# Context keys and values of the first attention for all heads at once, and three programs made into one

## The chip, the cores and the metric

The kernel runs on one core of a Trainium2 chip. The time is device time in microseconds (us) of one launch. TensorE (PE) does the matrix products, with its weight loads shown apart as PEld; VectorE (DVE), ScalarE (ACT) and GpSimd (POOL) do the rest; SyncE (SP) issues nearly all DMAs.

## The reference

Four residual steps over x of shape (4 sequences, 512 tokens, 512 wide), float32: an attention, a mixture of experts, a second attention and a quantised feed-forward. Only the first is touched. Cut to what matters:

```python
q = (x @ wq).reshape(B, L, 16, 128); k = (x @ wk).reshape(B, L, 4, 128); v = (x @ wv).reshape(B, L, 4, 128)
k_ctx = (h_ctx_kv @ wk_ctx).reshape(B, T, 4, 128)      # T = 64 context rows in each of 4 sequences
v_ctx = (h_ctx_kv @ wv_ctx).reshape(B, T, 4, 128)
q, k, k_ctx = rms_norm(q), rms_norm(k), rms_norm(k_ctx)
q, k = rope(q), rope(k)
k_full, v_full = concat([k_ctx, k]), concat([v_ctx, v])
out = softmax(q @ k_full.T * scale + causal) @ v_full    # 4 query heads to a key head
x = x + tanh(g_xattn[0]) * (out @ wo)                     # x in q, k, v is layernorm(x)
```

## The kernel before

The program is a row of stages with a barrier of all engines between two. The first three are `constants_stage` (loads an identity matrix, two masks and the gates, and takes the gates' tanh), `norm_transpose_stage` (loads x, normalises its 16 row tiles of 128 tokens on DVE and POOL, turns each on PE and stores it on ACT as `xT`) and `attention0_stage`.

`attention0_stage` goes through 64 slots: 4 key heads (a group of 16 slots each), in a group 4 sequences ("batches"), in a batch 4 tiles of 128 query tokens. A tile of place 0 to 3 in its batch has 192, 320, 448 or 576 keys. In each slot every engine does a fixed list of short steps; the lists are written out as strings (`PE_ORDER`, `ACT_ORDER`, `DVE_ORDER`, `POOL_ORDER`), one string for each place in the batch. A step belongs to a tile of its own: in slot s PE makes the scores of tile s (`S0` to `S3`, one for each query head, L746), turns the probabilities of tile s-1 (`P`, L793), multiplies them by the values (`V`, L803), projects tile s-2 back (`W`, L120 to L122 with `a_oth`), makes keys and values of tile s+2 (`k`, L765), its queries (`q`, L120 to L122 with `a_xch`) and turns keys and queries of tile s+1 (`K` L809, `T` L814). An engine never takes a step ahead of its order: it waits on semaphores and everything listed behind waits too.

Matmuls of queries and output are done in three passes of a rounded part and a rest. The weights' rounded part is made by ACT (`w`, L512, `a_whi`), the rest by POOL (`w`, L667, `a_wlo`); x likewise (`x`, L520 and L672). Squares for the norm of queries and keys are taken by ACT (`f`, L566), summed by DVE (`E`, L646), and POOL makes the factor and applies it (`q`, L676 to L684).

The context takes two PE steps in each batch: `C` in the slot of place 1 (L773, keys and values of the context of the next batch for this one key head), and `Y` in the slot of place 2 (L820, turns the 64 keys), with the steps `c` on ACT, DVE and POOL and `y` on ACT between. Their PSUM banks are handed out in turn with those of the other steps (`A_USE`, `TR_USE`). Ahead of the slots stand the loads, the tables of the rotation (DVE L578 to L584, once all of `tab_loaded` has landed) and slots -4 to -1, which fill the pipeline.

SP issues DMAs in program order, among them `load_piece` and `store_tern`, by which a later stage's weights are read in 256 KB pieces and turned to ternary in DVE's and ACT's `j` steps.

Of the kernel before, what the change touches and what calls it, by code (L numbers as in the profile page):

```python
# [124 lines left out]
def norm_transpose_stage(nc, stage, x, ident, x_in, xT, xn_dram):  # L125


    with ExitStack() as ctx:
        s = Scope(nc, ctx, stage)
        xn = s.sb("xn", [P, 2, D])  # L130
        stats = s.sb("stats", [P, 2, 6])
        mv = s.sb("mv", [P, 2, 2])
# [2321 lines left out]
```

## Time and profile before

| | us |
|---|---|
| median of 3 runs | 2126.61 (2123.35 to 2128.16) |
| the profiled execution, its own time | 2126.97 |
| its span, first to last instruction | 2125.2 |
| first scores of slot 0 start | 78.89 |
| first scores of slot 3 start | 122.24 |
| last scores of the first attention start | 1156.1 |

Busy shares of the span: PE 90%, PEld 64%, DVE 52%, ACT 49%, POOL 46%. A PE that is busy isn't at its peak, since matmul ends are modelled, so a stretch is judged by when steps start. All start times below count from the start of the span.

### The profile page before, as it was taken

Reading aid. Unit: us, or ns where it says so; the run is one execution under the profiler, and the core shown is the slowest. Engines: PE = TensorE matmul, PEld = TensorE weight load, DVE = VectorE, ACT = ScalarE, POOL = GpSimd, SP = SyncE. Lnnn points to the kernel's source line nnn. Section 1 sums busy time; section 2 is a strip of 40 time slices with the busy share of each in tenths; the row PEclk is TensorE's granted clock in tenths of the full one; section 3 lists DMA queues with packets and bytes.
Section 4 is the critical chain, followed back from the end, with each engine's and each line's share of the span. In section 5 each row is a group of like instructions: output and inputs, shape, how many; then the busy total and the mean of one; then the engine's idle time right before and its main releaser. Section 6 shows DMA issues by size and latency. Waiting matters only on the chain. (4 is left out here: it accounts for less than half of the span.)

```text
span 2125.2 us, 27622 instructions
## 1 busy us (share of the span) xinstructions
PE 1912.4 (90%) x9644; PEld 1360.0 (64%) x9644; DVE 1111.3 (52%) x2279; ACT 1050.3 (49%) x2303; POOL 980.0 (46%) x904
## 2 busy tenths in 40 slices
PE   3799999999999999999999799998999768859998
PEld 2567666666666666666666677777999646634443
DVE  4334434346446654455443546723444468747886
ACT  2456545654544444544454321115566256647775
POOL 1544444445445443554342100006888435537774
PEclk9999999999999999999999799999999979979999
DMA  3221211201012111111000410035889570000000
GB/s 120 65 65 48 62 35 30 65 19 55 25 35 65 45 58 28 36 46 43 16 1 1 148 55 21 21 121 167 231 224 257 144 188 1 1 0 16 21 21 26
DMA packets 112198, 139.58 MB, mean 66 GB/s; under 512 B 34864, under 2 KB 68656, under 8 KB 111872
## 3 DMA queue, kind: packets, MB, share of 16 engines
q1 hardware_dynamic: 104896, 121.06, 18.6%
q0 software_dynamic: 7168, 16.78, 3.8%
q8 instruction: 78, 1.28, 0.3%
q14 instruction: 56, 0.46, 0.1%
HBM read 104.26 MB, written 28.31 MB: 62 GB/s over the span
## 5 line engine op out<-in xcount | busy, mean ns | idle before, releaser
L672 POOL TENSOR_TENSOR a_xcl<-xT,a_xch 128x512 fp32r<-128x512 f32 x64 | 82.5, 1289 | 478.5 <-ACT a_xch L520 478.5
L803 PE MATMUL a_A<-a_pT,a_vf 128*128 128x512 f32 (+1 forms) x448 | 237.5, 612 | 1.4 <-ACT a_pT L533 1.2
L590 DVE TENSOR_REDUCE a_nmax<-a_S 128x1 f32<-128x192 f32 (+3 forms) x256 | 138.9, 553 | 186.2 <-PE a_S L747 186.1
L746 PE MATMUL a_S<-a_kT,a_qT 128*128 128x288 f32 (+3 forms) x640 | 212.2, 430 | 2.8 <-ACT a_pr_even L523 1.6
L120 PE MATMUL a_A<-a_wlo,a_xch 128*128 128x512 f32 x256 | 151.7, 593 | 31.1 <-DVE a_qb L634 23.2
L523 ACT ACTIVATE a_pr_odd<-a_S,a_nmax 128x320 f32<-128x320 f32 (+1 forms) x128 | 80.9, 633 | 185.4 <-DVE a_nmax L590 184.1
L533 ACT ACTIVATE a_pT<-a_TR 128x512 f32<-128x512 f32 (+1 forms) x224 | 132.9, 594 | 57.9 <-PE a_TR L793 57.5
L746 PEld LDWEIGHTS a_S<-a_kT,a_qT 128*128 128x128 f32 x640 | 121.1, 192 | 56.2 <-issue 28.8
L523 ACT ACTIVATE a_pr_even<-a_S,a_nmax 128x192 f32<-128x192 f32 (+1 forms) x128 | 67.0, 525 | 149.4 <-DVE a_nmax L590 149.3
L765 PE MATMUL a_A<-a_wkv,xT 128*128 128x256 f32 x512 | 134.9, 386 | 0.7 <-DMA a_wkv<-in_L_xattn_wv_dram 0.7
L1403 POOL TENSOR_TENSOR e_wlo<-expert_raw,e_whi 128x1408 fp32r<-128x1408 f32 x32 | 102.5, 3224 | 66.8 <-ACT e_whi L1476 66.8
L2274 PE MATMUL f_HH<-w12T,f_xqT 128*128 128x512 bf16 x512 | 122.1, 388 | 5.0 <-DVE f_xqT L2226 4.1
L627 DVE TENSOR_TENSOR a_otl<-a_A,a_oth 128x512 fp32r<-128x512 f32 x64 | 44.3, 692 | 157.3 <-ACT a_oth L537 157.3
L120 PE MATMUL a_A<-a_wlo,a_oth 128*128 128x512 f32 x256 | 113.1, 442 | 14.5 <-POOL a_wlo L667 8.3
L120 PE MATMUL e_GUP<-e_xgl,e_whi 128*128 128x256 f32 (+1 forms) x384 | 110.1, 287 | 5.3 <-DVE e_xgl L1519 4.5
L120 PEld LDWEIGHTS a_A<-a_wlo,a_xch 128*128 128x128 f32 x256 | 49.0, 191 | 100.6 <-issue 94.3
L2125 POOL TENSOR_TENSOR f_hg<-f_h,g 128x512 f32<-128x512 f32 x64 | 81.6, 1274 | 59.2 <-DVE f_h L2233 59.2
L121 PE MATMUL e_GUP<-e_xgh,e_wlo 128*128 128x256 f32 (+1 forms) x384 | 108.7, 283 | 0.0
L122 PE MATMUL e_GUP<-e_xgh,e_whi 128*128 128x256 f32 (+1 forms) x384 | 108.1, 281 | 0.0
L122 PE MATMUL a_A<-a_whi,a_xch 128*128 128x512 f32 x256 | 102.1, 399 | 0.0
L122 PE MATMUL a_A<-a_whi,a_oth 128*128 128x512 f32 x256 | 101.8, 398 | 0.0
L121 PE MATMUL a_A<-a_whi,a_xcl 128*128 128x512 f32 x256 | 101.6, 397 | 0.0
(368 smaller groups left out, 5115.7 us busy)
## 6 DMA issues: line engine op xcount, KB each, us to landing
a_pw<-in_L_ffn_w_dram SPq DMA_DIRECT2D x96, 256.0 KB, 2.8
expert_raw<-in_L_ffn_w_gate_dram SPq DMA_DIRECT2D x16, 704.0 KB
expert_raw<-in_L_ffn_w_up_dram SPq DMA_DIRECT2D x16, 704.0 KB
expert_raw<-in_L_ffn_w_down_dram SPq DMA_DIRECT2D x16, 512.0 KB
tern<-a_tern SPq DMA_DIRECT2D x48, 128.0 KB, 1.7
x_res<-in_x_dram SPq DMA_DIRECT2D x4, 1024.0 KB, 9.8
a_raw<-in_L_xattn_wq_dram SPq DMA_DIRECT2D x4, 1024.0 KB, 5.6
a_raw<-in_L_xattn_wo_dram SPq DMA_DIRECT2D x4, 1024.0 KB, 5.3
```

The source lines that it names most:

```text
L120: pe.matmul(out, lhs_hi, rhs_lo, start=first, stop=False)
L121: pe.matmul(out, lhs_lo, rhs_hi, start=False, stop=False)
L122: return pe.matmul(out, lhs_hi, rhs_hi, start=False, stop=last)
L523: act.activation(pr[s % 2][:, i, 0:keys(s)], pair(s, i), ACT.Exp, bias=nmax[:, s % 2, i:i + 1], accum_out=rs[:, s % 2, i:i + 1]).then_inc( ...
L533: act.activation(pT[0:rows(i), i % 2], TR[0:rows(i), TR_USE["P", t, i][0]], ACT.Copy).then_inc(pT_ready, 1)
L590: ve.tensor_reduce(nmax[:, s % 2, i:i + 1], pair(s, i), AX.X, ALU.max, negate=True).then_inc(s_max, 1)
L672: pool.tensor_tensor(xcl[:, t % 2], xT[:, :, tok(t)], xch[:, t % 2].bitcast(F32), ALU.subtract).then_inc(xlo_ready, 1)
L746: pe.matmul(bank[:, lo:hi], qT[:, t % 2, hq], kT[:, par(t), lo:hi], start=True, stop=hi < nk)
L765: last = pe.matmul(bank, xT[:, k, tok(t)], wkv[:, k].rearrange("p a n -> p (a n)"), start=k == 0, stop=k == KD - 1)
L803: last = pe.matmul(A[:, A_USE["V", t, 0][0]], vf[r, par(t), i], pT[r, i % 2], start=i == 0, stop=i == nkt - 1)
L1403: pool.tensor_tensor(wlo[e % 2][q, cs], raw[q, e % 2, cs], whi[e % 2][q, cs].bitcast(F32), ALU.subtract).then_inc(gu_lo, 1)
L2274: last = pe.matmul(HH[:, n % 2, j], xqT[:, u, j * KD + k], w12T[j][:, k, part(n)], start=k == 0, stop=k == KD - 1)
```

## The change

The two programs ahead of the attention are gone: their loads and steps are in the attention's own lists, in slots -3 to 10. The context's keys and values are made once, for all four key heads and sequences: `C` (keys) and `G` (values) are two steps each of four 512-column matmuls, `H` turns the keys, and both results are stored to DRAM (`ctx_keys`, `ctx_values`). At the second slot of a batch SP loads 64 columns of keys and 64 rows of values for the next batch. `C`, `Y`, `c` and `y` leave the repeating lists. The norm of x becomes `A` (DVE), `r` (POOL, ACT), `X` (DVE) and `R` (PE, turning): rows 0 to 3 in slot -3, one row in each later slot up to 10. Cut to its core:

```diff
-    PE_ORDER = ("S0 W0 W1 S1 W2 W3 P0 k0 S2 k1 P1 V0 q0 P2 V1 S3 P3 K V2 q1 T P4 V3 q2 V4 q3",
-                "S0 W0 W1 S1 W2 W3 P0 k0 S2 k1 C P1 V0 S3 K q0 T V1 q1 q2 q3",
-                "S0 W0 W1 S1 W2 W3 P0 k0 S2 k1 P1 Y V0 q0 S3 P2 V1 K q1 T V2 q2 q3",
-                "S0 W0 W1 S1 W2 W3 P0 k0 S2 k1 P1 V0 q0 P2 V1 S3 P3 K V2 q1 T V3 q2 q3")
...
-    POOL_ORDER = ("w x q p0 p1", "x q p0 p1 c", "w x q p0 p1", "x q p0 p1")
+    PE_ORDER = {-3: "Z0 Z1 R0 R1 R2 R3 C0 C1",
+                -2: "k0 k1 H0 q0 q1 q2 q3 H1",
+                -1: "k0 k1 G0 R K T q0 q1 q2 q3 G1",
+                0: "S0 W0 W1 S1 W2 W3 P0 k0 S2 R k1 P1 V0 q0 P2 V1 S3 P3 K V2 q1 T P4 V3 q2 V4 q3",
+                1: "S0 W0 W1 S1 W2 W3 P0 k0 S2 R k1 P1 V0 S3 K q0 T V1 q1 q2 q3",
+                2: "S0 W0 W1 S1 W2 W3 P0 k0 S2 R k1 P1 V0 q0 S3 P2 V1 K q1 T V2 q2 q3",
+                3: "S0 W0 W1 S1 W2 W3 P0 k0 S2 R k1 P1 V0 q0 P2 V1 S3 P3 K V2 q1 T V3 q2 q3"}
+    ACT_ORDER = {-3: "z0 z1 r0 r1 r2 r3 x c0",
+                 -2: "w c1 x v h0 f h1",
+                 -1: "x v d0 r k t f y d1",
+                 0: "w x e0 j0 e1 g0 j1 e2 v r g1 n g2 j2 e3 g3 k t g4 o f",
...
+    DVE_SLOT = "M0 M1 N0 D X j0 M2 N1 v N2 j1 M3 N3 B E A"
+    DVE_ORDER = {-3: "A0 A1 X0 A2 X1 A3 X2 X3 t c0 c1", -2: "v E A", -1: "v X E A", 0: DVE_SLOT, 1: DVE_SLOT, 2: DVE_SLOT, 3: DVE_SLOT}
+
+    POOL_ORDER = {-3: "r0 r1 r2 r3 x c0", -2: "w c1 x r", -1: "x q r", 0: "w x q p0 p1 r", 1: "x q p0 p1 r", 2: "w x q p0 p1 r", 3: "x q p0 p1 r"}
...
+    def row(s, ahead, i):
+        return i if s == BEGIN else s + ahead if BT <= s + ahead < PERIOD else None
...
+                sp.dma_start(ident[:], consts["ident"]).then_inc(ident_loaded, 16)
+                load_x(0)
+                sp.dma_start(ctx_raw, ctx_in.rearrange("b t d -> (b t) d").rearrange("(t p) d -> p t d", p=P)).then_inc(ctx_loaded, 16)
+                sp.dma_start(wkc, wkc_in.rearrange("(k p) n -> p k n", p=P)).then_inc(wkc_loaded, 16)
                 load_q(0)
+                sp.dma_start(wrow[:, 1], kw_in.partition_broadcast(P)).then_inc(tab_loaded, 16)
                 load_pair(0, wkv, wk_in, wv_in, wkv_loaded)
+                sp.dma_start(wrow[:, 0], qw_in.partition_broadcast(P)).then_inc(tab_loaded, 16)
+                for n in "kq":
+                    sp.dma_start(cw[n][:], consts["cos"].rearrange("(t p) d -> p t d", p=P)).then_inc(tab_loaded, 16)
+                    sp.dma_start(sw[n][:], consts["sin"].rearrange("(t p) (s d) -> p t s d", p=P, s=2)).then_inc(tab_loaded, 16)
+                for k in range(KD):
+                    sp.dma_start(wvc[k], wvc_in[k * P:(k + 1) * P]).then_inc(wvc_loaded, 16)
+                sp.dma_start(causal_in[:], consts["causal"]).then_inc(causal_loaded, 16)
+                sp.dma_start(graw[:, :, 0], g_xattn.partition_broadcast(P), allow_slow_non_contiguous=True).then_inc(gates_loaded, 16)
+                sp.dma_start(graw[:, :, 1], g_ffn.partition_broadcast(P), allow_slow_non_contiguous=True).then_inc(gates_loaded, 16)
+                for b in range(1, B):
+                    load_x(b)
+                sp.dma_start(tri[:], consts["tri"]).then_inc(tri_loaded, 16)
                 load_piece(0)
                 load_piece(1)
-                for s in range(BEGIN, SLOTS):
+                store_keys(0)
+                sp.wait_ge(ck_stored, 16)
+                load_keys(0)
+                store_keys(1)
+                sp.wait_ge(wlo_ready, 4)
+                load_o(0)
+                store_values(0)
+                sp.wait_ge(cv_stored, 16)
+                load_values(0)
+                store_values(1)
+                sp.wait_ge(ck_stored, 32)
+                sp.wait_ge(cv_stored, 32)
+                    if s % BT == 1 and live(s, BT - 1):
+                        t = batch_next(s)
+                        if t >= 2 * BT:
+                            sp.wait_ge(o_full, tile(t - BT - 1))
+                        load_keys(t // BT)
+                        load_values(t // BT)
...
+                    if name == "A" and row(s, 6, i) is not None:
+                        t = row(s, 6, i)
+                        u = t % 2
+                        if t % BT == 0:
+                            ve.wait_ge(x_loaded[t // BT], 16)
+                        ve.bn_stats(stats[:, u], x[:, t]).then_inc(x_stats, 1)
+                        ve.wait_ge(x_stats, 2 * t + 1)
+                        ve.bn_aggr(mv[:, u], stats[:, u]).then_inc(x_stats, 1)
+                        ve.wait_ge(x_stats, 2 * t + 2)
+                        ve.tensor_scalar(veps[:, u:u + 1], mv[:, u, 1:2], 1e-5, None, ALU.add).then_inc(x_var, 1)
+                    if name == "X" and row(s, 5, i) is not None:
+                        t = row(s, 5, i)
+                        u = t % 2
+                        ve.wait_ge(x_rstd, t + 1)
+                        if t > 1:
+                            ve.wait_ge(xn_turned, t - 1)
+                        ve.tensor_scalar(xn[:, u], x[:, t], mv[:, u, 0:1], rstd[:, u:u + 1], ALU.subtract, ALU.mult).then_inc(xn_ready, 1)
+                    if name == "t":
...
+                    if name == "c":
+                        ve.wait_ge(ck_sq, i + 1)
+                        ve.tensor_reduce(ssc[:, i], csq, AX.X, ALU.add).then_inc(ck_sum, 1)
+                        ve.tensor_tensor(kc[:, i], A[:, A_USE["C", i, 0][0]].rearrange("p (h d) -> p h d", h=KVH),
+                                         kw[:].unsqueeze(1).broadcast_to([P, KVH, HD]), ALU.mult).then_inc(ck_done, 1)
...
+                    if name == "c":
+                        pool.wait_ge(ck_sum, i + 1)
+                        pool.tensor_tensor(msc[:, i], ssc[:, i], heps[:, 0:KVH], ALU.add).then_inc(ck_ms, 1)
+                        pool.wait_ge(ck_ms, i + 1)
+                        pool.tensor_tensor(src[:, i], msc[:, i], mhalf[:, 0:KVH], ALU.pow).then_inc(ck_rs, 1)
+                        pool.wait_ge(ck_done, i + 1)
+                        pool.wait_ge(ck_rs, i + 1)
+                        pool.tensor_tensor(kc[:, i], kc[:, i], src[:, i].unsqueeze(2).broadcast_to([P, KVH, HD]), ALU.mult).then_inc(ck_ready, 1)
...
+                    if name == "C":
+                        pe.wait_ge(wkc_loaded, 16)
+                        pe.wait_ge(ctx_copied, i + 1)
+                        bank = bank_of_A("C", i, s, m)
+                        for k in range(KD):
+                            last = pe.matmul(bank, ctxT[:, k, i * P:(i + 1) * P], wkc[:, k], start=k == 0, stop=k == KD - 1)
+                        last.then_inc(ck_full, 1)
+                    if name == "G":
+                        pe.wait_ge(wvc_loaded, 16 * KD)
+                        bank = bank_of_A("G", i, s, m)
+                        for k in range(KD):
+                            last = pe.matmul(bank, ctxT[:, k, i * P:(i + 1) * P], wvc[k], start=k == 0, stop=k == KD - 1)
+                        last.then_inc(cv_full, 1)
+                    if name == "H":
+                        pe.wait_ge(ck_ready, i + 1)
+                        bank = bank_of_TR("H", i, 0, s, m)
+                        for h in range(KVH):
+                            last = pe.transpose(bank[:, h * P:(h + 1) * P], kc[:, i, h], ident[:])
+                        last.then_inc(ck_turned, 1)
+                    if name == "R" and row(s, 5, i) is not None:
...
-                    if name == "C":
-                        bank = bank_of_A("C", t, s, m)[:, 0:2 * HD]
-                        if t % PERIOD == 0:
-                            until(pe, wc_loaded, lambda v: 32 * (v // PERIOD + 1), t, m)
-                        for k in range(KD):
-                            last = pe.matmul(bank, ctxT[:, k, ctx_tok(t)], wc[:, k].rearrange("p a n -> p (a n)"), start=k == 0, stop=k == KD - 1)
-                        last.then_inc(c_full, 1)
...
```

POOL, from the first step on x to the first queries' norm, before: `a_msc`, `a_src` and `a_kc` are the context step `c`, `a_wlo` the rest of the query weights, `a_msq` to the last `a_qa` the norm of queries of tile 0.

```order
L672 TENSOR_TENSOR a_xcl<-xT,a_xch 128x512
L693 TENSOR_TENSOR a_msc<-a_ssc,a_heps 64x1
L695 TENSOR_TENSOR a_src<-a_msc,a_mhalf 64x1
L697 TENSOR_TENSOR a_kc<-a_kc,a_src 64x128
L667 TENSOR_TENSOR a_wlo<-a_raw,a_whi 128x512 x4
L672 TENSOR_TENSOR a_xcl<-xT,a_xch 128x512 x2
L676 TENSOR_TENSOR a_msq<-a_ssq,a_heps 128x5
L678 TENSOR_TENSOR a_srq<-a_msq,a_mhalf 128x5
L681 TENSOR_TENSOR a_qa<-a_qa,a_qb 128x640
L684 TENSOR_TENSOR a_qa<-a_qa,a_srq 128x640
```

And with the change, from the same step to the same norm; `a_rstd` is the norm of a row of x, and `a_msc`, `a_src`, `a_qT` the context step `c`, now on 128 rows and 4 heads.

```order
L680 TENSOR_TENSOR a_xcl<-xT,a_xch 128x512
L700 TENSOR_TENSOR a_msc<-a_ssc,a_heps 128x4
L702 TENSOR_TENSOR a_src<-a_msc,a_mhalf 128x4
L705 TENSOR_TENSOR a_qT<-a_qT,a_src 128x512
L675 TENSOR_TENSOR a_wlo<-a_raw,a_whi 128x512 x4
L700 TENSOR_TENSOR a_msc<-a_ssc,a_heps 128x4
L702 TENSOR_TENSOR a_src<-a_msc,a_mhalf 128x4
L705 TENSOR_TENSOR a_qT<-a_qT,a_src 128x512
L680 TENSOR_TENSOR a_xcl<-xT,a_xch 128x512
L668 TENSOR_TENSOR a_rstd<-a_veps,a_mhalf 128x1
L680 TENSOR_TENSOR a_xcl<-xT,a_xch 128x512
L684 TENSOR_TENSOR a_msq<-a_ssq,a_heps 128x5
```

The context step now stands twice, on either side of the weights' rest, and a step of the row norm stands ahead of the x tile that the queries' norm follows.

PE in slot 1, from the first turned probabilities to the turned keys, before (`a_wc` is the step `C`):

```order
L793 MATMUL a_TR<-ident_f,a_pr_even 128x128 x4
L765 MATMUL a_A<-a_wkv,xT 128x256 x2
L746 MATMUL a_S<-a_kT,a_qT 128x320
L747 MATMUL a_S<-a_causal,a_ident_b 128x128
L765 MATMUL a_A<-a_wkv,xT 128x256 x2
L773 MATMUL a_A<-a_wc,a_ctxT 128x256 x4
L793 MATMUL a_TR<-ident_f,a_pr_even 128x128 x4
L803 MATMUL a_A<-a_pT,a_vf 128x512
L746 MATMUL a_S<-a_kT,a_qT 128x320
L747 MATMUL a_S<-a_causal,a_ident_b 128x128
L809 MATMUL a_TR<-ident_f,a_qa 128x128
```

And with the change (`a_xn` is the step `R`):

```order
L822 MATMUL a_TR<-ident_f,a_pr_even 128x128 x4
L801 MATMUL a_A<-a_wkv,xT 128x256 x2
L780 MATMUL a_S<-a_kT,a_qT 128x320
L781 MATMUL a_S<-a_causal,a_ident_b 128x128
L762 MATMUL a_TR<-ident_f,a_xn 128x128 x4
L801 MATMUL a_A<-a_wkv,xT 128x256 x2
L822 MATMUL a_TR<-ident_f,a_pr_even 128x128 x4
L832 MATMUL a_A<-a_pT,a_vf 128x512
L780 MATMUL a_S<-a_kT,a_qT 128x320
L781 MATMUL a_S<-a_causal,a_ident_b 128x128
L838 MATMUL a_TR<-ident_f,a_qa 128x128
```

The four passes of the context step are gone from between the second half of `k` and the second `P`, and the four transposes of a row of x stand ahead of that half.

## Rows read from the trace of the kernel before

**Rows 1.** Windows: length, busy of PE, PEld, DVE, ACT, POOL; PEclk; DMA share, GB/s.

```profile
0.00:78.89 78.89, 35.10 (x127) 26.13 (x127) 29.17 (x88) 19.16 (x39) 23.44 (x34) 0.96 0.40 124
78.89:122.24 43.35, 37.82 (x163) 25.69 (x162) 17.82 (x46) 23.82 (x66) 26.25 (x28) 0.95 0.13 43
122.24:1169.00 1046.76, 1002.55 (x4510) 698.48 (x4509) 511.49 (x1086) 527.67 (x1353) 479.79 (x486) 0.99 0.13 38
1169.00:2125.20 956.20, 836.94 (x4848) 609.70 (x4846) 552.85 (x1060) 479.63 (x846) 450.53 (x356) 0.94 0.32 92
```

**Rows 2.** Windows of slot 5 and of slot 61, first scores to first scores.

```profile
156.99:172.44 15.45, 15.24 (x71) 11.08 (x69) 7.63 (x18) 9.14 (x28) 7.88 (x10) 1.00 0.18 53
...
1119.57:1133.30 13.73, 13.52 (x63) 9.56 (x62) 7.35 (x17) 6.33 (x18) 5.56 (x6) 1.00 0.01 1
```

**Rows 3.** Timeline, PE, slots 5 and 6: start, length, line, operation, tiles.

```profile
164.27 1.89 PE L773 MATMUL a_A<-a_wc,a_ctxT 128*128 128x256 f32 x8
165.99 0.60 PE L793 MATMUL a_TR<-ident_f,a_pr_even 128*128 128x128 f32 x4
166.52 1.12 PE L803 MATMUL a_A<-a_pT,a_vf 64*128 64x512 f32 x2
...
179.97 0.60 PE L793 MATMUL a_TR<-ident_f,a_pr_odd 128*128 128x128 f32 x4
180.50 0.27 PE L820 MATMUL a_TR<-ident_f,a_kc 64*128 64x64 f32 x1
180.61 1.07 PE L803 MATMUL a_A<-a_pT,a_vf 64*128 64x512 f32 x2
```

**Rows 4.** Timeline of the first two programs and the start of the third.

```profile
0.73 0.40 SPq L2310 DMA_DIRECT2D ident_f<-const_ident_dram  x1
...
7.51 2.60 SPq L152 DMA_DIRECT2D x_res<-in_x_dram  x4
...
13.13 1.29 DVE L175 BATCH_NORM_STATS2 n_stats<-x_res 128x6 f32 x2 [5.48 <-DMA x_res<-in_x_dram]
...
15.04 1.17 POOL L198 TENSOR_TENSOR n_rstd<-n_veps,n_mhalf 128x1 f32<-128x1 f32 x2 [14.61 <-DVE n_veps L182]
...
45.21 0.31 ACT L497 ACTIVATE a_ident_b<-ident_f 128x128 bf16<-128x128 f32 x1 [0.78 <-PEq L100]
```

**Rows 5.** Timeline from the landing of the tables to the first scores.

```profile
53.24 0.23 DVE L578 TENSOR_SCALAR a_kw<-a_sq 128x128 f32<-128x128 f32 x1 [7.51 <-DMA a_sq<-in_L_xattn_k_norm_w_dram]
...
56.44 0.63 ACT L520 ACTIVATE a_xch<-xT 128x512 fp32r<-128x512 f32 x1 [4.65 <-DVE a_sin_k L584]
...
61.13 4.98 POOL L667 TENSOR_TENSOR a_wlo<-a_raw,a_whi 128x512 fp32r<-128x512 f32 x4
...
67.16 0.60 ACT L566 ACTIVATE a_sq<-a_A 128x512 f32<-128x512 f32 x1 [4.71 <-PE a_A L122]
...
67.79 0.82 DVE L646 TENSOR_REDUCE a_ssq<-a_sq 128x5 f32<-128x640 f32 x1 [4.93 <-ACT a_sq L566]
...
69.86 1.18 POOL L678 TENSOR_TENSOR a_srq<-a_msq,a_mhalf 128x5 f32<-128x5 f32 x1
...
72.61 1.25 POOL L684 TENSOR_TENSOR a_qa<-a_qa,a_srq 128x640 f32<-128x640 f32 x1
...
73.92 0.47 PE L809 MATMUL a_TR<-ident_f,a_qa 128*128 128x128 f32 x1 [3.04 <-POOL a_qa L684]
...
78.89 0.73 PE L746 MATMUL a_S<-a_kT,a_qT 128*128 128x192 f32 x2
```

**Rows 6.** Windows of 2 KB loads, of 512-byte loads, and ahead of the first scores.

```profile
11.00:20.00 9.00, 2.17 (x9) 1.77 (x10) 5.23 (x16) 1.19 (x2) 2.34 (x4) 1.00 1.03 387
49.20:53.20 4.00, 1.96 (x8) 1.56 (x8) 0.00 (x0) 1.19 (x2) 0.00 (x0) 1.00 1.21 297
72.60:79.40 6.80, 5.48 (x16) 4.46 (x17) 0.26 (x1) 1.15 (x3) 1.25 (x1) 0.50 0.00 0
```

**Rows 7.** The page, DMA issues: the 256 KB pieces.

```profile
a_pw<-in_L_ffn_w_dram SPq DMA_DIRECT2D x96, 256.0 KB, 2.8
```

More of the change, by code:

```diff
@@ L392, in attention0_stage @@
+        ck_stored, cv_stored, ck_loaded, cv_loaded = (s_.sem(n) for n in ("ck_stored", "cv_stored", "ck_loaded", "cv_loaded"))
         q_sq, q_sum, q_rot, q_ms, q_rs, q_add, q_ready = (s_.sem(n) for n in (
             "q_sq", "q_sum", "q_rot", "q_ms", "q_rs", "q_add", "q_ready"))
-        c_ms, c_rs, c_ready = s_.sem("c_ms"), s_.sem("c_rs"), s_.sem("c_ready")
         piece_loaded = [s_.sem(f"piece_loaded{u}") for u in range(2)]
@@ L657, in _ @@
             def _(pool):
-                pool.wait_ge(tab_ready, 4 + 2 * (1 + BT))
+                pool.wait_ge(tab_ready, 2)
                 def do(name, i, s, m):
+                    if name == "r" and row(s, 6, i) is not None:
+                        t = row(s, 6, i)
+                        pool.wait_ge(x_var, t + 1)
+                        pool.tensor_tensor(rstd[:, t % 2:t % 2 + 1], veps[:, t % 2:t % 2 + 1], mhalf[:, 0:1], ALU.pow).then_inc(x_rstd, 1)
                     if name == "w" and s % PERIOD in (2, 14):
@@ L716, in bank_of_A @@
                         sem, count = {"W": (wo_done, tile), "V": (o_lo, tile), "q": (q_rot, tile), "k": (kv_done, tile),
-                                      "C": (c_done, batch)}[before[0]]
+                                      "C": (ck_done, tile), "G": (cv_copied, tile)}[before[0]]
                         until(pe, sem, count, before[1], m)
@@ L724, in bank_of_TR @@
                         sem, count = {"P": (pT_ready, turn(before[2])), "T": (qT_ready, tile), "K": (kT_ready, tile),
-                                      "Y": (cT_ready, batch)}[before[0]]
+                                      "Z": (ctx_copied, tile), "R": (xT_ready, tile), "H": (ck_copied, tile)}[before[0]]
                         until(pe, sem, count, before[1], m)
@@ L740, in do @@
                             if t % BT == 0:
-                                until(pe, cT_ready, batch, t, m)
+                                until(pe, ck_loaded, lambda v: 16 * batch(v), t, m)
+                                pe.wait_ge(tab_ready, 3)
                         until(pe, s_exp, head(i - 2), t, m)
@@ L799, in do @@
                             if t % BT == 0:
-                                until(pe, c_done, batch, t, m)
+                                until(pe, cv_loaded, lambda v: 16 * batch(v), t, m)
                         until(pe, pT_ready, turn(i), t, m)
@@ L2330, in build @@
         ident = sb(ctx, "ident_f32", [P, P])
-        causal = sb(ctx, "causal_f32", [P, P])
         tri = sb(ctx, "tri_f32", [P, P])
```

331 lines of the change are left out of this document (124 added, 207 removed), and 9 rows, old and new, of tables (ACT_ORDER, DVE_ORDER).

## Prediction

> **What bounds the kernel now.** I read the windows first, cut where the scores of slots 0 and 3 begin and where the first attention ends. From 122.24 to 1169 us PE is busy 1002.55 of 1046.76 us at a mean clock of 0.99, while no other engine reaches 530 us there [rows 1]; the reader is to see one full engine beside four half-empty ones. In this stretch a step that leaves PE is worth the distance between the starts of its neighbours. The first 78.89 us are the other kind: PE is busy 35.10 of them, and what ends a wait there is a landing, DVE or POOL in turn [rows 1, 4, 5]. The 956.20 us behind the attention are untouched. Then I read slot against slot in the windows, the lead step by step in the timeline, and the rates of loads in the windows again.
>
> **The steady slots.** The trace holds the experiment for step C. Slot 5 has it and takes 15.45 us; slot 61, the same place in its batch with no batch to follow, lacks it and takes 13.73 us [rows 2]. The difference, 1.72, is also the distance from C's first pass to the next step, 164.27 to 165.99 [rows 3]. C stands in 15 slots (1, 5, ... 57); I count 14 here and slot 1 below: 14 x 1.71 = 23.9 us gained. Slot 61 also shows that nothing else fills the place: without C it is idle only 0.21 of its 13.73 us, as slot 5 is of its 15.45 [rows 2]. What could take part of it back is the bank: the queries' first product then waits for DVE's key step of the same slot, and in the slots with ternary pieces DVE is later. Bounds: none of 1.71 lost, or all of it in the 6 such slots (10 us); slot 61 is nearest and I take none.
>
> Step Y is cheap: from the turned probabilities to the values it is 0.53 us without it (165.99 to 166.52) and 0.53 + 0.11 with it (179.97 to 180.61) [rows 3]. 14 x 0.11 = 1.5 us gained. The small steps c and y on ACT, DVE and POOL go too; these engines have spare time [rows 1], so I count them at nothing.
>
> Against that, R, A, X and r of rows 5 to 15 of x now lie in slots 0 to 10. R is four transposes as in the turning of probabilities, 0.53 us from start to next step [rows 3]; in slots 3 to 10, with PE full, 8 x 0.53 = 4.2 us lost. A is about 1 us on DVE (13.13 to 15.04 for two rows) and r 0.6 us on POOL [rows 4], at the end of a slot, ahead of the next maxima. DVE's half-empty slots [rows 1] cover them; without the cover each would delay the exponentials and so PE, at most 1 us x 8. Below, the wait where q0 waits for DVE may shrink by as much as R adds; I keep 4.2, between 0 and 12.
>
> The loads of stored keys and values are issued by SP three slots ahead of their use. A 256 KB piece lands 2.8 us after its issue [rows 7], a slot lasts 13.7 to 15.5 us [rows 2], so I count them at nothing.
>
> **The lead.** Before: 78.89 us to the first scores. After, on the order of each engine:
>
> 1. Data. One queue brings everything in program order. Up to the causal mask, for which DVE's table step waits, stand 4.5 MiB in 2 KB rows (first quarter of x, context, three weights) and 1.75 MiB in 512-byte rows. At 387 and 297 GB/s [rows 6] these are 12.2 and 6.2 us. The lead of a load: x is issued from 7.51 and its first MiB is there at 13.13 [rows 4]; 5.6 less 2.7 of transfer leaves 2.9. From the first issue at 0.73 [rows 4]: 0.73 + 2.9 + 18.4 = 22.0 us.
> 2. Tables: 53.24 to 56.44, 3.2 us [rows 5], so 25.2.
> 3. POOL's order, shown above, puts c0 ahead of the weights' rest. DVE sums the squares of four heads, 0.7 us (four fifths of 0.82), and multiplies; POOL's power of four columns takes about 1.0 (1.18 for five) and a product 1.25 [rows 5]. c0 ends near 28.5.
> 4. The rest of the query weights: 4.98 us [rows 5], 33.5. From its end to the squares of the queries it was 67.16 - 66.11 = 1.05 [rows 5], so f starts at 34.5.
> 5. From f to the end of the queries' norm it was 67.16 to 73.86, 6.7 us [rows 5]. Now POOL first takes c1 (0.2 + 1.0 + 1.25, to 36), an x tile, and then r of row 4, for which DVE's E and A must end (34.5 + 0.6 + 2.0 + 1.0 = 38.2). With r 0.6 and another x tile of 1.3 the norm starts near 40 and takes 4.2: 44.3. So K starts about 3 us later than the old pattern would have it.
> 6. From K to the first scores it was 73.92 to 78.89, 4.97 us [rows 5], at half clock (0.50 in 72.6 to 79.4, the engine having waited 3.04 us for POOL ahead of it [rows 5, 6]); about 3.6 at full. G1 now lies in between: twice the columns of C, 2 x 1.72 = 3.4 us at full clock [rows 3], 6.9 at half. So the first scores start at 51.4 us with a full clock and 56.2 with a half one.
>
> The Trainium skill, "TensorE: Matmul & The Clock Gate", section Part 1 on the HAM clock gate, says that the array is throttled unless recent activity has released it. The trace agrees (0.50 behind a wait of 3.04 us), and by that rule the lead, in which PE mostly waits, would end at the later of the two times.
>
> I take 54: half of the stretch slow. H, k and G0 lie in POOL's shadow; if POOL were quicker, G0 (3.4) would come into the path. Gain 78.89 - 54 = 24.9 us, bounds 22.7 and 27.5. Slots 0 to 2 took 43.35 us [rows 1]. They lose C once but gain three R, and A delays the maxima in slot 1, where PE already waits; I take 0.8 us lost, from 2 gained to 4 lost.
>
> **Sum.** 24.9 - 0.8 + 23.9 + 1.5 - 4.2 = 45.3 us. The profiled execution took 2126.97 us, 0.36 above the median of 2126.61, so 2081.7 by the one and 2081.3 by the other; I write 2081.
>
> **Rivals.** First, the setup is slower than I have it: the causal mask at the end of the load queue, POOL's one list and a half clock add up, or the row norm's DVE steps reach PE in slots 1 to 10. For it: six waits in a row hang on the order of POOL and SP, and one late landing moves all. Price: 2.2 more for the later of the two leads, 3.2 for slots 0 to 2 at their bound, 4 for A in slots 3 to 10 (half of its bound), and 2.6 for a landing that comes a MiB later (1.05 MB at 387 GB/s): 2081 + 12 = 2093.
>
> Second, the setup is faster: the 512-byte rows too run at 387 GB/s (4.7 us for 6.2), the clock is full by K (2.6), and slots 0 to 2 end at their better bound (2.8). Together 7, so 2074. Against it: 297 GB/s was measured in just such a queue, and the half clock in just such a place [rows 6].
>
> Third, PE's time isn't given back, since DVE's key step ends the slot instead: the C term falls to 14 us and R stays, 2091, or at its worst 2105. Against it stands slot 61.
>
> On the other side: every batch waits for its keys. If SP, which runs one list with the pieces and ternary stores, reaches the load only when the batch is due, PE stands still at 15 batch starts for an issue and a landing, 2.8 us [rows 7]: 42 us, and 2123, no change that a measurement can tell. From 45.3 / 15 = 3.0 us each it is slower, and two loads one behind the other could cost that: 3.3 each gives 2131. Against it: the load hangs on values of a batch that ended three slots earlier, 40 us.
>
> The Trainium skill, "DMA: Bandwidth & Descriptors", section Anatomy of one DMA, puts a fixed 2 us on every DMA, and its specification table asks for 512 bytes for line rate, while a key load has 256 bytes to a partition. By its figures alone an exposed load would be an estimated 2.1 us and 15 of them 31; the 2.8 of the 256 KB pieces stands in its place here.
>
> **How the numbers follow.** The sum's own case 0.68 (2075 to 2089), slower setup 0.12, faster setup 0.10, PE's time not given back 0.05, waiting batches 0.05, of which 0.02 short of a measurable loss. Other stretches of half clock, each worth some 2 us, may move by one or two either way. The range takes in the sum, both setups and the milder end of the third: 2068 to 2095, about 0.9 of the cases by their middles, 0.8 with their spread. A measurement of this kernel can tell about 0.2%, 4 us, from no change: faster 0.95, same 0.02, slower 0.03.
>
> **What would show it.** Right: first scores near 54 us; slot 5 near 14.2 us and slot 13 near 13.7; the slots of places 0 and 3 unchanged behind slot 10; no wait of PE on `ck_loaded` or `cv_loaded`; the end of the attention some 45 us earlier and what follows as long as before. Wrong: a wait of PE ahead of the first score of a batch; slot 13 at 15.4 us; first scores beyond 60 us; the maxima of slots 3 to 10 so late that PE waits for exponentials; or another clock behind 1169 us.

## Result: faster, by half of what was predicted

The changed kernel took 2102.91 us (median of 4 runs, 2102.16 to 2105.11), the kernel before 2125.51 beside it (4 runs, 2123.35 to 2128.16): a ratio of 0.9895, interval 0.9878 to 0.9912. The prediction said 2081, with a range of 2068 to 2095; the sign was right, the gain 22.6 us in place of 45. In later series the kernel before stood at 2128.4 to 2129.3 and the changed one at 2102.2, so the gain is 23 to 27 us.

The windows of the changed kernel, cut at the first scores, at slot 3 and at the attention's end, answer to [rows 1]; the columns are the same:

```profile
0.00:55.92 55.92, 36.09 (x113) 22.84 (x114) 19.63 (x49) 15.37 (x30) 20.92 (x26) 0.88 0.67 218
55.92:104.98 49.06, 39.55 (x167) 27.01 (x165) 20.36 (x54) 24.55 (x65) 27.13 (x28) 0.90 0.14 45
104.98:1144.00 1039.02, 990.35 (x4423) 684.90 (x4422) 519.47 (x1104) 523.92 (x1306) 463.33 (x452) 0.99 0.13 37
1144.00:2101.20 957.20, 837.42 (x4841) 610.79 (x4839) 553.03 (x1060) 480.08 (x845) 450.84 (x356) 0.94 0.32 92
```

The reader sees a lead of 55.92 us for 78.89, slots 0 to 2 longer by 5.7, and a long third window only 7.7 shorter, where some 21 were expected. PE's work in it fell by 12.2 us (1002.55 to 990.35), not by the 14 x 1.7 of step C.

Yet step C is gone as predicted. The windows of slots 5 and 13 answer to [rows 2]:

```profile
141.28:155.66 14.38, 14.17 (x66) 9.96 (x65) 8.66 (x21) 9.14 (x26) 7.35 (x8) 1.00 0.19 61
273.21:287.00 13.79, 13.58 (x63) 9.57 (x61) 7.37 (x17) 6.87 (x19) 6.77 (x7) 1.00 0.15 44
```

14.2 and 13.7 were forecast. And nothing waits for the loads of stored keys and values: this is the whole list of PE's waits from 104 to 1144 us (total us, times, longest), without a DMA in it.

```profile
PE a_A L120 <- DVE a_qb L643: 26.5, 27, 1.6
PE a_A L120 <- POOL a_wlo L675: 6.1, 6, 1.9
PE a_A L120 <- issue: 5.3, 3, 1.8
PE a_A L120 <- DVE a_otl L636: 4.8, 17, 1.4
PE a_TR L843 <- ACT a_pT L526: 3.3, 16, 0.6
PE a_A L832 <- ACT a_pT L526: 1.2, 2, 0.9
PE a_TR L762 <- DVE a_xn L577: 1.1, 2, 0.6
```

Where the rest went is seen when slots are laid beside slots, before against after. Apart from step C and the rows of x, they differ only where one of the two shows half clock. Slots 24 and 32 are the same place with the same work; these are their windows in the changed kernel, and from its timeline the queries' first product in each:

```profile
454.85:474.44 19.59, 18.12 (x80) 12.82 (x79) 9.38 (x20) 7.78 (x21) 6.87 (x7) 0.91 0.14 41
593.33:611.21 17.88, 16.42 (x80) 11.85 (x79) 9.36 (x20) 7.78 (x21) 6.86 (x7) 1.00 0.15 44
```

```profile
464.22 0.47 PE L120 MATMUL a_A<-a_wlo,a_xch 128*128 128x512 f32 x1 [1.47 <-DVE a_qb L643]
...
602.68 0.47 PE L120 MATMUL a_A<-a_wlo,a_xch 128*128 128x512 f32 x1 [1.46 <-DVE a_qb L643]
```

Both slots have the wait for DVE's key product, 1.47 and 1.46 us. After the first, the granted clock is 0.50 for 3.4 us (1.2 GHz, the lower of its two levels, in place of 2.4), as a window of just this stretch shows; such stretches are called half clock below. The row above it is one of 6.8 us in slot 2, of which more below:

```profile
85.80:92.60 6.80, 5.46 (x12) 3.66 (x13) 0.70 (x2) 1.49 (x5) 6.72 (x7) 0.50 0.16 41
464.70:468.10 3.40, 3.40 (x9) 2.08 (x9) 0.61 (x1) 0.60 (x1) 0.00 (x0) 0.50 0.45 134
```

The slot's mean is 0.91, and PE is busy 1.7 us longer for the same 80 instructions; after the second it stays at full. In the kernel before both slots took 17.92 us. Before, four such stretches fell into slots 3 to 61 (14, 43, 51, 55); after, nine (24, 27, 30, 34, 46, two in 50, 52, 55).

The account from profile to profile, in us gained, with the start of slot 62 (1133.30 before, 1108.28 after) as the cut behind the slots:

| term | predicted | in the traces |
|---|---|---|
| lead, to the first scores | 24.9 | 23.0 |
| slots 0 to 2 | -0.8 | -5.7 |
| step C, 14 slots | 23.9 | 23.5 (14 x 1.68) |
| step Y | 1.5 | 0 |
| R, A, X, r in slots 3 to 10 | -4.2 | -5.0 |
| slots 3 to 61 whose clock differs | 0 | -10.4 |
| small lengthenings, up to 0.06 a slot | 0 | -0.3 |
| from slot 62 on (991.90 to 992.92) | 0 | -1.0 |
| sum (of unrounded terms) | 45.3 | 24.0 |

The -10.4 is the sum over ten slots whose clock differs: 14, 43 and 51 gained 1.47, 1.66 and 1.63; 24, 27, 30, 34, 46, 50 and 52 lost 1.67, 1.64, 1.50, 2.80, 1.55, 4.33 and 1.68. Slot 50 holds two stretches. Slots 34 and 50 lost more than their stretches because a second wait follows the first stretch there, which the kernel before does not have. These are the queries' first product of slot 34, the first ternary step (`j0`) that it waits behind, and the wait for DVE's key product in the kernel before, all slots together (27 times and 26.5 us with the change, above):

```profile
639.74 0.47 PE L120 MATMUL a_A<-a_wlo,a_xch 128*128 128x512 f32 x1 [1.62 <-DVE a_qb L643]
```

```profile
634.30 1.48 DVE L614 TENSOR_SCALAR a_below<-a_pw,a_nthr 128x512 bf16<-128x512 f32 x1
635.82 1.62 DVE L618 SCALAR_TENSOR_TENSOR a_tern<-a_pw,a_thr,a_below 128x512 bf16<-128x512 f32 x1
```

```profile
PE a_A L120 <- DVE a_qb L634: 23.2, 25, 1.5
```

In slot 34 of the kernel before the same two instructions took 0.48 and 0.75 us, and the queries' first product did not wait. Behind the half clock they start 1.2 us later in the slot and run beside POOL's products for the queries' norm; why that matters stands under "The waits away". So some 3 us of the 10.4 are these two waits, 1.62 in slot 34 and 1.42 in slot 50 (half clock follows the latter too), and the rest is the slower clock itself.

### The profile page after: what moved, and what is told of

It reads as the page before. It is cut to its first block and busy times, and to the rows that moved or that the text cites. A ratio compares the mean times of both kernels' runs of the same rounds, so it can differ in the third digit from the quotient of the medians.

```text
span 2101.2 us, 27108 instructions
## 1 busy us (share of the span) xinstructions
PE 1903.4 (91%) x9540; PEld 1345.5 (64%) x9540; DVE 1112.5 (53%) x2265; ACT 1043.9 (50%) x2245; POOL 962.2 (46%) x862
## 5 line engine op out<-in xcount | busy, mean ns | idle before, releaser
L120 PE MATMUL a_A<-a_wlo,a_xch 128*128 128x512 f32 x256 | 152.4, 595 | 32.1 <-DVE a_qb L643 26.5
L636 DVE TENSOR_TENSOR a_otl<-a_A,a_oth 128x512 fp32r<-128x512 f32 x64 | 44.3, 692 | 156.6 <-ACT a_oth L530 156.6
L801 PEld LDWEIGHTS a_A<-a_wkv,xT 128*128 128x128 f32 x512 | 89.1, 194 | 22.3 <-DVE a_qT L593 6.7
```

What stands on the lines that cost most here:

```text
L120: pe.matmul(out, lhs_hi, rhs_lo, start=first, stop=False)
L801: last = pe.matmul(bank, xT[:, k, tok(t)], wkv[:, k].rearrange("p a n -> p (a n)"), start=k == 0, stop=k == KD - 1)
```

## Experiments

All times are medians; slots with half clock are counted from 3 to 61, in one profiled execution of each kernel. Theory A: PE's longer waits are the old ones, and which of them half clock follows hangs on when they fall. Rival B: the absence of C's work brings the clock down at those places.

**A little more work at one place.** Ahead of step k in slot 12, products that the step then overwrites (n = 2, 4, 6):

```diff
+for _ in range(n if s == 12 and i == 0 else 0):
+    pe.matmul(bank, xT[:, 0, tok(t)], wkv[:, 0]..., start=True, stop=True)
```

> The changed kernel with two extra products of the first slice of x with the key and value weights in slot 12, ahead of step k, which then starts its bank afresh: 0.86 us more work on PE at one place, and the same result. Its profile should keep every wait of the changed kernel and every slot length but that of slot 12. Theory A (the waits of PE of 1.4 us and more are the old ones, and whether one of them is followed by 3.4 us of half clock hangs on the moment at which it falls): another set of slots behind slot 12 has half clock than 24, 27, 30, 34, 46, 50 (two), 52 and 55, in number 4 to 10, and the time is 2103.8 us plus 1.65 for each stretch above those 9, minus 1.65 for each below, so 2096 to 2105. Rival B (PE lost the work of step C, and its absence beside the waits brings the clock down in those places): the same slots have it, 2103.8 us, give or take 1.

> As the one before, with four extra products, 1.72 us in slot 12. Theory A: yet another set of slots with half clock, 4 to 10 of them, and 2104.6 us plus or minus 1.65 for each stretch above or below 9. Rival B: the same slots as in the changed kernel, 2104.6 us.

> As the shifts of 0.86 and 1.72 us, with six extra products, 2.58 us in slot 12. Theory A: another set of slots with half clock than in the changed kernel, 4 to 10 of them, and 2105.5 us plus or minus 1.65 for each above or below 9. Rival B: the nine of the changed kernel, 2105.5 us.

Measured 2099.6 (2099.0 to 2102.5), 2108.5 (2102.8 to 2109.1) and 2104.7 us (2100.3 to 2109.9). With 0.86 us of work added the median is 3 us lower, which the spread of the unchanged kernel's executions (2096.7 to 2108.4 us, below) does not let one call a gain. What the profile shows is where the half clock stands. The windows of its slots 24, 27 and 43:

```profile
455.32:473.24 17.92, 16.46 (x81) 11.86 (x79) 9.38 (x20) 7.76 (x21) 6.87 (x7) 1.00 0.15 45
...
503.36:524.64 21.28, 19.60 (x82) 13.54 (x81) 11.75 (x21) 9.07 (x20) 7.85 (x7) 0.92 0.12 37
...
780.50:801.74 21.24, 19.57 (x83) 13.55 (x82) 11.74 (x21) 9.07 (x20) 7.84 (x7) 0.92 0.14 38
```

Slot 24 now runs at full clock, 43 does not: six stretches (27, 30, 34, 43, 46, 50). Slot 62 starts 4.3 us earlier for it (1103.95 for 1108.28), and what follows takes 3.8 us longer (996.7 for 992.9). The third shift has five (24, 35, 43, 46, 50). The second alone speaks for B: it has the nine of the changed kernel, and another in slot 14 beside them. The first and third contradict B.

**The same kernels again.**

> The changed kernel, unchanged, profiled in another execution. Theory A: the same slots at full clock, another set with half clock than 24, 27, 30, 34, 46, 50 (two), 52 and 55, or a part of them; 5 to 10, 2098 to 2106 us. Rival B: the same nine. If the median comes out at 2102 to 2104 again, the distance to the kernel before on the same chip, 2129, is 25 to 27 us.

> The kernel before, unchanged, profiled in another execution. Theory A (which of the same waits is followed by half clock hangs on when it falls): every slot at full clock takes what it took in the first profile, within 0.05 us, but the slots with half clock behind slot 3 are not 14, 43, 51 and 55 again; between 3 and 10 of them, and the time 2121 to 2135 us. Rival B (the work beside the waits decides): the same four.

2102.2 (2096.7 to 2108.4) and 2128.4 us (2124.6 to 2137.8). The changed kernel's slots 24, 27 and 36 in this execution:

```profile
451.81:471.35 19.54, 18.09 (x81) 12.98 (x80) 9.36 (x20) 7.77 (x21) 6.86 (x7) 0.91 0.13 41
...
501.50:521.11 19.61, 17.94 (x82) 12.60 (x81) 11.73 (x21) 9.08 (x20) 7.86 (x7) 1.00 0.14 41
...
662.73:682.32 19.59, 18.14 (x81) 12.82 (x79) 9.37 (x20) 7.77 (x21) 6.87 (x7) 0.91 0.14 41
```

Slot 27 is at full clock and 36 is not; there are eight stretches (24, 30, two in 34, 36, 39, 46, 50). One program, two executions, two sets: B in its strict form is out. The kernel before changed less than A expected: 18 in place of 14, and 43, 51 and 55 again. Between these two profiles slot 62 starts 27.6 us earlier with the change (1131.34 to 1103.71), for 25.0 in the first pair.

**C's time back, without C.** The same dead products, four of them, in the 15 slots that had C (`i == 0 and 1 <= s <= 57 and s % BT == 1`).

> The changed kernel with four extra products (of x's first slice with the key and value weights, a bank that step k then starts afresh) ahead of step k in the 15 slots of place 1 that had step C: PE's time of C back, without C's loads, statistics or turning; the result is the same. Slots of place 1 return to 15.4 to 15.5 us, so 15 x 1.72 = 25.8 us more at full clock. Theory A with the spacing of the waits as what decides: the stretches in slots 3 to 62 come back to what the kernel before has, 4 to 7, and the time is 2120 to 2127 us. If the number has to do with anything else of the change: 9 or 10, 2128 to 2131.

2115.7 us (9 runs, 2107.0 to 2126.3): 25.8 us of added work cost 13.5. Slots 24, 25 and 43:

```profile
461.24:479.14 17.90, 16.45 (x81) 11.86 (x80) 9.36 (x20) 7.76 (x21) 6.86 (x7) 1.00 0.14 45
479.14:494.63 15.49, 15.28 (x71) 11.08 (x69) 10.54 (x21) 6.84 (x19) 7.32 (x7) 1.00 0.18 57
...
788.91:810.19 21.28, 19.60 (x82) 13.51 (x81) 11.75 (x21) 9.08 (x20) 7.84 (x7) 0.92 0.14 37
```

Slot 25 has its old length, and three stretches are left, in 43, 51 and 55: the very slots of both profiles of the kernel before. That points to C's time in the rhythm of the slots, and not to its loads, statistics or turning; but it is one profile, and the nine executions lie 19 us apart, at mean clocks from 0.957 to 0.968. A had expected 4 to 7 stretches. The median lies below the expected 2120 to 2127: slot 1, which waits anyway, took up its products (14.44 us, and 14.45 at full clock without them in the third shift), and the execution profiled, 2118.3, lies above the median.

**C away, and nothing else.**

```diff
-if name == "c" and live(batch_next(s), 0):
+if name == "c" and batch_next(s) < 2 * BT:
```

(the same for y, C and Y, and for the waits on them).

> The kernel before with steps C, Y, c and y left out from the third batch on, and the loads of the next heads' context weights with them (the later batches then read the contexts' keys and values of the first two, so this part of the computation is left out): the one part of the change that gave the prediction its largest term, alone, with the two programs and the lead of before. Both theories: 13 slots of place 1 fall from 15.44 to 13.76 us, 21.8 us, and the lead and slots 0 to 4 stay as they were. Theory A (which waits are followed by half clock hangs on when they fall): the number of such stretches in slots 3 to 62 differs from the 4 of before, anything from 3 to 10, and the time is 2107 us plus 1.65 for each above 4, so 2105 to 2117. Rival D (the added half clock comes from what else the change did: rows normalized beside the slots, loads of stored keys): 4 stretches, 2105 to 2107.

2112.4 us (2105.4 to 2117.0). Slots 13 and 24:

```profile
284.64:298.36 13.72, 13.51 (x62) 9.55 (x61) 7.35 (x17) 6.85 (x19) 6.75 (x7) 1.00 0.13 38
...
467.55:487.12 19.57, 18.10 (x80) 12.78 (x79) 9.38 (x20) 7.76 (x21) 6.87 (x7) 0.91 0.12 41
```

C's time is given back, and the stretches go from four to six (14, 24, 27, 30, 34, 51), 24, 27, 30 and 34 among them as in the changed kernel. Rival D, something else in the change, needed the four old ones and 2105 to 2107 us: the set and the median are against it. The execution profiled is the fastest of the five, though, and its 2105.4 us alone would fit D.

**The waits away.** In slots 24 to 55 the waits for DVE's key product come from DVE's first ternary step, which stands ahead of it. The step is long there. These are the first and the second ternary step of slot 32 in the changed kernel:

```profile
597.83 1.37 DVE L614 TENSOR_SCALAR a_below<-a_pw,a_nthr 128x512 bf16<-128x512 f32 x1
599.24 1.62 DVE L618 SCALAR_TENSOR_TENSOR a_tern<-a_pw,a_thr,a_below 128x512 bf16<-128x512 f32 x1
...
602.52 0.47 DVE L614 TENSOR_SCALAR a_below<-a_pw,a_nthr 128x512 bf16<-128x512 f32 x1
603.02 0.75 DVE L618 SCALAR_TENSOR_TENSOR a_tern<-a_pw,a_thr,a_below 128x512 bf16<-128x512 f32 x1
```

The first runs while POOL makes its products for the queries' norm (597.38 to 600.32), the second while POOL rests. In this trace all 24 ternary steps beside a resting POOL took 0.47 and 0.75 us. So the wait of 1.46 us hangs on what POOL does at the time as well as on the order; no run varied POOL alone. The step was moved back in places 0, 2 and 3 (with one wait of DVE on its own last step):

```diff
-M0 M1 N0 D X j0 M2 N1 v N2 j1 M3 N3 B E A
+M0 M1 N0 D X M2 N1 v N2 j0 j1 M3 N3 B E A
```

> The changed kernel with DVE's first ternary step of a slot (j0) moved behind the key's products and N2 in the slots of places 0, 2 and 3 (and a wait of DVE on its own last ternary step ahead of the next). In slots 24 to 55 the queries' first product waits 1.46, 0.68 and 1.5 us for DVE's key product, which stands behind j0. Theory A: without these waits 16 slots lose 0.7 to 1.5 us each, some 16 to 20 us, and the half clock that followed them in slots 24, 27, 34, 50, 52 and 55 goes too, 5 to 6 stretches of 1.65 us: 2075 to 2082 us. Rival B (half clock comes from what PE lacks since step C went, whatever waits there are): the waits go, the stretches stay, 2083 to 2087. Rival C (the two ternary steps one behind the other make the last head's maxima late, and PE waits for that instead): 2095 or more.

> The kernel before with the same change of DVE's order as in the late ternary step: j0 behind N2 in places 0, 2 and 3. Theory A: the waits of 1.46 and 1.5 us in slots 24 to 55 go, 12 slots lose 1.25 to 1.5 us, 16 us, and the half clock in slots 43, 51 and 55 with them, 5 us: 2105 us or so (2101 to 2111). Beside the changed kernel with the same order, 2078.8, the change is then worth more than the 25 us that its attention gained in the profile: the scores of slot 63 should start 30 to 33 us earlier in the one trace than in the other, since neither is left with more than 1 to 3 stretches in slots 3 to 62. Rival B (the missing work of C brings half clock): the distance between the two stays at 25 us.

2078.8 us (2077.2 to 2080.7) for the changed kernel, 2112.5 (2107.4 to 2117.0) for the one before. Slots 24 and 27, first of the changed kernel so ordered, then of the kernel before:

```profile
453.95:470.38 16.43, 16.43 (x81) 11.86 (x80) 8.05 (x20) 7.97 (x21) 6.30 (x7) 1.00 0.16 49
...
500.46:518.82 18.36, 17.93 (x83) 12.60 (x82) 10.21 (x21) 9.07 (x20) 7.66 (x7) 1.00 0.14 43
```

```profile
474.56:490.98 16.42, 16.42 (x81) 11.85 (x79) 8.09 (x20) 7.97 (x21) 6.33 (x7) 1.00 0.17 48
...
522.73:541.08 18.35, 17.91 (x83) 12.59 (x82) 10.20 (x21) 9.07 (x20) 7.66 (x7) 1.00 0.14 44
```

These waits are gone from both, and with them all stretches of the changed kernel but two (30, 46); the kernel before keeps three (18, 34, 46), more than the expectation's 2105 us had room for. The change is now worth 33.7 us by the medians, and slot 62 starts 34.4 earlier (1114.64 to 1080.26), against 25.0 with the waits. That is the direct evidence that half clock, with the waits that it brings, ate this part: where the slots whose clock differs come out nearly even (0.5 us for the changed kernel in place of 10.4 against it), the same change gives 9 us more. Rival B fails. Rival C fails by the time, but has a point: in slots 34 and 50 of the changed kernel, and in 50 of the one before, the turning of the queries now waits 1.58 and 1.56 us behind ACT's copy of the probabilities, and the slot takes 20.1 us for 18.45 at the same full clock.

**Rows of x earlier.** DVE's step A from the slot's end to behind N2, and the norm ahead of the key's product in the last program ahead of slot 0:

```diff
-DVE_SLOT = "M0 M1 N0 D X j0 M2 N1 v N2 j1 M3 N3 B E A"
+DVE_SLOT = "M0 M1 N0 D X j0 M2 N1 v N2 A j1 M3 N3 B E"
--1: "v X E A"
+-1: "X v E A"
```

> The changed kernel with DVE's statistics of a row of x (step A) between N2 and the maxima of the last head instead of at the slot's end, and the row's norm (X) ahead of the key's product in the last program ahead of slot 0. Theory: A at the end of a slot delays the maxima of the next and, through POOL's power r, which stands ahead of the weights' rest, the first output projection. Then slot 1 falls from 15.5 to 14.5 us or less, the wait for the weights' rest in slot 2 from 4.9 to about 2 and slot 2 from 23.7 to 20 us, slots 4 and 8 lose their wait of 0.57 for the row's norm, and the first scores come 1.2 us earlier, near 54.7: 6 to 8 us in all, so about 2096 us, give or take 8 for stretches of half clock that then fall elsewhere behind slot 12. Rival (the order of POOL and the late landing of the weights set slot 2 whatever DVE does): slot 2 stays at 23 us or more, and the gain is the 2 us of the lead and slot 1 at most.

2097.1 us (2085.6 to 2100.1). This is why slot 2 was long; the timeline of the changed kernel shows A, the power r, the weights' rest and the output projection that waits for it:

```profile
84.04 0.69 DVE L566 BATCH_NORM_STATS2 a_stats<-x_res 128x6 f32<-128x512 f32 x1
...
85.21 0.56 POOL L668 TENSOR_TENSOR a_rstd<-a_veps,a_mhalf 128x1 f32<-128x1 f32 x1 [7.93 <-DVE a_veps L570]
85.73 4.96 POOL L675 TENSOR_TENSOR a_wlo<-a_raw,a_whi 128x512 fp32r<-128x512 f32 x4
...
87.14 0.77 PE L120 MATMUL a_A<-a_wlo,a_oth 128*128 128x512 f32 x1 [4.90 <-POOL a_wlo L675]
```

With A earlier POOL doesn't stand in r when the weights come:

```profile
78.54 5.00 POOL L675 TENSOR_TENSOR a_wlo<-a_raw,a_whi 128x512 fp32r<-128x512 f32 x4 [4.99 <-ACT a_whi L500]
...
79.96 0.47 PE L120 MATMUL a_A<-a_wlo,a_oth 128*128 128x512 f32 x1 [1.84 <-POOL a_wlo L675]
```

Slot 2 falls from 23.70 to 18.79 us and slot 1 from 15.50 to 13.74, as the theory has it, the half clock in both included; slots 4 and 8 keep a wait of 0.44. The first scores come at 53.57, but only about 1 us of that is the norm's: the turned keys start at 45.19 for 46.17, and the rest is 3.4 us less of half clock. Of these 10 us the median shows 5 to 6: the profile has ten stretches behind slot 3, slot 14 and the old nine, and takes 3 us longer behind slot 62; one execution took 2085.6 us, at a mean clock of 0.963 for 0.957 to 0.959 in the other five.

**Both, and PE's order in seven slots.** The two orders of DVE together; then also

```diff
+PE_NEW_O = "S0 S1 P0 W0 W1 W2 W3 k0 S2 R k1 P1 V0 q0 S3 P2 V1 K q1 T V2 q2 q3"
+PE_NEW_Q = "S0 W0 W1 S1 W2 W3 P0 k0 S2 R k1 P1 V0 S3 P2 q0 V1 K q1 T V2 q2 q3"
```

the first in slots 2, 18, 34 and 50, the second in 14, 30 and 46.

> The changed kernel with both orders of DVE: the statistics of a row ahead of the last head's maxima, the norm ahead of the key's product in the last program ahead of slot 0, and the ternary steps behind N2. If the two losses are apart, as the theory has it: 2097.1 less 24.1, so 2073, give or take 4 for stretches of half clock behind the attention; first scores at 53.6, slots 0 to 2 near 42.4 us, slots 24 and 27 at 16.4 and 18.4. Rival (the gains overlap, since each moved the same stretches): 2079 or more.

> The one before with another order of PE in two slots of every sixteen: in slots 2, 18, 34 and 50 the second head's scores and the first turning of probabilities stand ahead of the output projection, which waits 1.84 us for the new weights' rest there; in slots 14, 30 and 46 the last head's scores and the third turning stand ahead of the queries' first product, which waits 1.77 us. Theory A: seven waits shrink to 0.4 us, 9 to 10 us, and the last stretches of half clock in slots 3 to 62 go, 2 or 3 of 1.65: 2060 us (2057 to 2066). Rival (the steps moved ahead are late themselves, or the projection's bank is then the wait): 2070 or more.

2068.4 us (2067.7 to 2070.8) and 2060.6 us (2054.7 to 2062.4; ratio to the kernel before 0.9669, interval 0.9652 to 0.9686). The gains add up, with 4.6 us more than the expected 2073; the kernel with the two orders starts its scores at 52.27 us, though slots 0 to 2 still take 45.3, with half clock in 1 and 2, where 42.4 was expected. With the third order slots 14 and 18 look like this, and no slot from 3 to 61 has half clock:

```profile
276.52:292.61 16.09, 15.74 (x69) 10.36 (x67) 7.12 (x16) 9.91 (x23) 12.27 (x11) 1.00 0.21 66
...
341.13:359.15 18.02, 16.70 (x69) 10.05 (x68) 7.04 (x16) 11.63 (x29) 12.11 (x11) 1.00 0.32 99
```

Slot 14 waits 0.35 us, from 1.78. Slot 18 came down by only 0.43 (18.45 to 18.02): the wait is spread over the four pieces of the weights, 1.3 in all for 2.07, so the expected 0.4 held in three slots of seven, 14, 30 and 46. It is the best kernel of the study and lies 42 us under the changed one.

## Why the prediction was wrong, and where it was right

**Step C.** Right: 23.9 predicted, 23.5 in the trace. DVE's key step did not take the place over (rival three): PE idles 0.21 us in slot 13 as before.

**Half clock.** This is the step that failed: "Other stretches of half clock, each worth some 2 us, may move by one or two either way." It put the net number at none, and the sum has no term for it. In the first pair of profiles there are five more, and the slots whose clock differs lost 10.4 us. The price of one was nearly right (1.5 to 1.7, and 2.8 in slots 34 and 50, where a second wait follows it), the number wasn't, and the argument had no ground for it: the trace of before holds 18 waits of 1.4 us and more in slots 3 to 61, and half clock behind four of them only. I treated the four as a property of the slots; they are one of the draws. What the runs show beyond that is a tendency. Profiles in which place 1 keeps C's time and the ternary waits stand have three or four stretches (both of the kernel before, and the one with dead products); the seven that lack C's time have 5 to 10. The shorter rhythm fares worse in these ten profiles. Why it does is open: the runs show that the moment of a wait matters, not what about the moment.

The Trainium skill, "TensorE: Matmul & The Clock Gate", section Part 1 on the HAM clock gate, says that what the gate goes by runs freely and isn't set anew when a kernel starts. The two executions of the changed kernel agree with it: slots 27 and 52 at half clock in one, 36 and 39 in the other.

**Slots 0 to 2.** The term was mis-sized, -0.8 with a bound of -4 for -5.7. I had A delay the maxima of slot 1, and it did, PE's wait there growing from 1.23 to 2.24 us. What I missed is POOL's list: r at the end of slot 1 stands ahead of w in slot 2, so the weights' rest waits for A as well, and the output projection 4.90 us for 1.84. With that wait came 6.8 us of half clock, from 85.8, and 3.4 in slot 1. The earlier A takes all of this back, 42.37 us for the three slots against 43.35 before the change, and so shows it.

**The lead.** 54 predicted, 55.92 in the first profile, 53.66 in the second. Its steps, from the timeline: causal mask, weights' rest, squares, the queries' norm, the row's norm, R, K, first scores.

```profile
22.58 0.23 DVE L580 CAST a_causal<-a_causal_f 128x128 bf16<-128x128 f32 x1 [9.08 <-DMA a_causal_f<-const_causal_dram]
...
29.13 4.99 POOL L675 TENSOR_TENSOR a_wlo<-a_raw,a_whi 128x512 fp32r<-128x512 f32 x4
...
35.16 0.60 ACT L551 ACTIVATE a_sq<-a_A 128x512 f32<-128x512 f32 x1 [2.90 <-PE a_A L122]
...
43.67 1.26 POOL L692 TENSOR_TENSOR a_qa<-a_qa,a_srq 128x640 f32<-128x640 f32 x1
43.83 1.37 DVE L577 TENSOR_SCALAR a_xn<-x_res,a_mv,a_rstd 128x512 f32<-128x512 f32 x1
...
45.26 1.12 PE L762 MATMUL a_TR<-ident_f,a_xn 128*128 128x128 f32 x4 [2.84 <-DVE a_xn L577]
46.17 0.42 PE L838 MATMUL a_TR<-ident_f,a_qa 128*128 128x128 f32 x1
...
55.92 0.49 PE L780 MATMUL a_S<-a_kT,a_qT 128*128 128x192 f32 x2
```

22.0, 28.5, 34.5 and 44.3 were worked out for the mask, the start of the weights' rest, the squares and the end of the norm; the trace has 22.6, 29.1, 35.2 and 44.9. The 0.6 of the first landing runs through unchanged. Not counted was R of row 4, which stands ahead of K on PE and waits for a norm that DVE reaches only at 43.83: K starts at 46.17 in place of 44.9, 1.2 us. With the norm ahead of the key's product K starts at 45.19. From K to the first scores the prediction had 7.1 us at full clock and took 9.7, with half of the stretch slow; it was 9.75 in the first profile, with 6.8 us of half clock from 44.9, and 7.61 in the second, with none. So the half share met the first execution by luck, and the two leads of one program, 2.3 us apart, differ by 2.1 us in this stretch. The order's own worth is seen where neither has half clock there: 53.66 in the second profile, 52.27 with both orders, 1.4 us.

**Step Y** gave nothing: the slots of place 2 at full clock take 15.71 us before and after. Its 0.11 us between two starts was taken up by what follows. **R and its kin** cost 5.0 for 4.2, well within their bounds, 2.9 of it in slots 4 and 8, where PE waits 0.57 for the row's norm.

**The other rivals.** The slower setup came in part (1.9 in the lead, 4.9 more in slots 0 to 2). No batch waits for its loads, which land 1.7 us (keys) and 1.9 us (values) after their issue by the medians, where the prediction had 2.8 from the pieces and an estimate of 2.1. What follows the attention is the same work, but its clock is drawn anew too: from slot 62 on it took 990.5 to 998.6 us over these profiles, so that the -1.0 of the first pair is a draw as well. Two small slips in the prediction's sums change nothing: 1.05 MB at 387 GB/s is 2.7 us and not 2.6, and the wait for E and A ends at 38.1 and not 38.2.

## What to carry to other kernels

Where an engine is full but for short waits, price a removed step at the distance between its neighbours, and then ask what the shorter rhythm does to the clock: waits of 1.5 us that cost nothing more today may each cost twice that tomorrow. Take such waits away first, here by moving a step that nobody waits for behind one that PE waits for; the change was worth 25 us beside them and 34 without. And with a step moved to the end of an engine's slot, read what stands at the head of its next slot on every engine that it feeds.

## What the runs showed of the hardware that I had not expected

Added work can be cheaper than its own time: 25.8 us of dead products cost 13.5 us by the medians. Half clock comes with waits as short as 1.42 us (slot 50 of the changed kernel), always for 3.4 us in slots 3 to 61, and the same wait in the same place brings it in one execution and not in another. DVE's ternary step takes 0.47 and 0.75 us beside a resting POOL and up to 1.48 and 1.63 beside POOL's products. So single executions of one program lie far apart: 2085.6 to 2100.1 us, 2107.0 to 2126.3 us. A profile's clock is one draw, and a gain of 10 us read from one profile of each kernel can be that draw.
